# Attention scores by pairs of heads in two 64-row chunks, row maxima from the first chunk alone

## The reference

```python
x = x + tanh(g_xattn) * xattn(layernorm(x), ctx, ctx)            # softmax(q k^T / 4) v, 16 heads
x = x + tanh(g_ffn) * ffn(layernorm(x))
# in ffn: attn = softmax(rope(q) rope(k)^T / 4); sa = (attn v) Wo; x = rmsnorm(src + sa) * norm1_w
# then shared SwiGLU + two of eight experts per token, and a second rmsnorm
```

## Time and profile before

| | us |
|---|---|
| median of 3 runs | 788.73 (787.22 to 789.63) |
| profiled execution, its own time | 793.59 |
| its span, first to last instruction | 791.8 |
| first unit's exponential starts | 55.2 |
| last unit's exponential starts | 535.1 |
| TensorE clock, mean of full | 0.986 |

### The profile page before, as it was taken

The page is one execution under the profiler, slowest core; times in us unless marked ns, Lnnn a source line. Parts: engine busy times, 40 slices in busy tenths (PEclk is TensorE's granted clock), DMA queues, the critical chain, the costliest instruction groups (busy, mean ns, idle before and its releaser), DMA issues.

```text
span 791.8 us, 10350 instructions
## 1 busy us (share of the span) xinstructions
PE 746.5 (94%) x3510; PEld 342.7 (43%) x3510; DVE 512.4 (65%) x777; ACT 408.1 (52%) x766; POOL 225.6 (28%) x342
## 2 busy tenths in 40 slices
PE   5889999999999999999999999999999999989994
PEld 3432343243233233233323423425645755458883
DVE  2588847956978878878797798743366022623764
ACT  2437867777767767876675777683211122222000
POOL 3360222314315405304222410010105622400654
PEclk9989999999999999999999999999999999999997
DMA  7792334216215414513411341006003734000010
GB/s 233 207 256 57 81 84 144 79 32 204 63 50 164 122 41 126 141 41 94 146 43 40 125 112 47 1 2 213 0 0 125 272 115 133 0 1 1 34 41 34
DMA packets 51892, 73.31 MB, mean 93 GB/s; under 512 B 7808, under 2 KB 42880, under 8 KB 51840
## 3 DMA queue, kind: packets, MB, share of 16 engines
q1 hardware_dynamic: 47248, 63.80, 27.4%
q0 software_dynamic: 2816, 8.46, 2.8%
q10 hardware_dynamic: 1776, 0.40, 0.3%
HBM read 45.04 MB, written 27.33 MB: 91 GB/s over the span
## 4 chain that ended last, share of the span: by engine, by line
PE 75%; DVE 14%; ACT 5%; issue 3%; DMA 1%; POOL 1%; ACTq 0%; DVEq 0%; POOLq 0%
PE ps L1483 35%; PE ps L1629 12%; PE ps L1653 11%; PE ps L1603 10%; DVE negm L1136 7%; ACT hS L891 3%; PE ps L1478 2%; DVE bst L1014 2%; PE ps L1617 1%; PE ps L1542 1%; DMA bv_bc<-in_L_xattn_bv_dram 1%; PE ps L1537 1%; PE ps L1563 0%; POOL out_dram L753 0%; DVE rows L1021 0%
## 5 line engine op out<-in xcount | busy, mean ns | idle before, releaser
L1136 DVE TENSOR_REDUCE negm<-ps 128x2 f32<-128x1024 f32 x256 | 304.0, 1221 | 75.8 <-PE ps L1603 68.0
L891 ACT ACTIVATE hS<-ps 128x512 f32<-128x512 f32 x512 | 280.6, 604 | 116.2 <-PE ps L1653 114.4
L1653 PE MATMUL ps<-w 98*128 98x512 bf16 x512 | 170.6, 386 | 4.8 <-DVE qk L1069 1.9
L1603 PE MATMUL ps<-w 96*128 96x512 bf16 x512 | 154.9, 383 | 7.3 <-DVE negm L1136 6.4
L1629 PE MATMUL ps<-hS,mix 128*17 128x512 f32 x1024 | 134.7, 598 | 0.2
L1653 PEld LDWEIGHTS ps<-w 98*128 98x128 bf16 x512 | 44.0, 97 | 157.0 <-ACT hS L891 76.7
L1603 PEld LDWEIGHTS ps<-w 96*128 96x128 bf16 x512 | 47.9, 99 | 59.7 <-DVE negm L1136 13.2
L1335 DVE SCALAR_TENSOR_TENSOR ctxs<-qk,ps 128x512 f32<-128x512 f32 x32 | 22.0, 688 | 76.3 <-ACT qk L925 51.1
L925 ACT ACTIVATE qk<-ps 128x512 f32<-128x512 f32 x32 | 19.1, 597 | 82.5 <-PE ps L1483 78.6
L1483 PE MATMUL ps<-w,hS 128*128 x256 | 55.7, 379 | 2.0 <-issue 2.0
L1483 PEld LDWEIGHTS ps<-w,hS 128*128 128x128 f32 x256 | 48.6, 190 | 9.4 <-issue 2.9
(11 more groups left out here) (210 smaller groups left out, 875.5 us busy)
## 6 DMA issues: line engine op xcount, KB each, us to landing
w<-scrq SPq DMA_DIRECT2D x32, 384.0 KB, 4.5
scrk<-mix SPq DMA_DIRECT2D x24, 256.0 KB, 2.1
scrq<-mix SPq DMA_DIRECT2D x16, 384.0 KB, 3.3
scrq<-mix SPq DMA_DIRECT2D x24, 256.0 KB, 2.5
w<-scrk SPq DMA_DIRECT2D x32, 192.0 KB, 2.9
w<-scrk SPq DMA_DIRECT2D x32, 128.0 KB, 2.9
w<-in_L_ffn_W_experts_dram SPq DMA_DIRECT2D x8, 512.0 KB, 8.0
mix<-scrf SPq DMA_DIRECT2D x4, 528.0 KB, 5.5
```

The lines of the kernel that those rows point to most:

```text
L891: nc.scalar.activation(prob[:, kt % PROB_SLOTS, s % HG, :], slot_bank(("unit", u)), ACT.Exp, scale=SC).then_inc(s_exp, 1)
L1136: V.tensor_reduce(negm[:, gi % 2, h, 2 * t2:2 * t2 + 2], ps[:, bank:bank + 2, :], AX.X, ALU.max, negate=True).then_inc(s_re, 1)
L1603: last = MM(ps[:, bank + t, :], qs[0:STK, g, h, tt * P:(tt + 1) * P], ks[0:STK, g, h, :], start=True, stop=True)
L1653: MM(take(("unit", u)), ks[:, g, h, kt * P:(kt + 1) * P], qs[:, g, h, :], start=True, stop=True).then_inc(s_sT, 1)
```

## The change

Each unit's score becomes two accumulating matmuls over 64 and 34 rows, and two heads are taken together: the even head of a pair lies in partitions 0 to 63, the odd one in 64 to 127, so their matmuls use the upper and the lower half of the array and two different banks. The first chunk holds terms 0 to 3 (the larger ones in the new order of `Q_PART` and `K_PART`), the second terms 4 and 5 and the two maximum rows (for the even head it runs over 64 rows, zeros and ones included). The maxima come from the first chunk alone, for two heads and one tile of queries: two matmuls, each into its own bank, and DVE reduces each bank in an instruction of 128 x 512. There are four score banks (0, 1, 7, 5), and three banks for maxima (2, 3, 4), each single. `scrk` gets all six terms, stacks are loaded in eight DMAs a group instead of four, the set-up memsets cover other rows (SP waits for the first of them), the hook lists and three of the fixed steps are new.

```diff
-Q_PART = [0, 0, 0, 1, 1, 2]
-K_PART = [0, 1, 2, 0, 1, 0]
+Q_PART = [1, 1, 0, 0, 0, 2]
+K_PART = [1, 0, 1, 0, 2, 0]
+HALF = 64
 LEAD = 12
 PROB_SLOTS = 3
-AT_COPY, AT_HEADS, AT_MAX, AT_ROWS = 4, 8, 9, 11
-SCORE_BANKS = [0, 1, 7]
+AT_COPY, AT_HEADS, AT_MAX, AT_ROWS = 3, 9, 10, 11
+SCORE_BANKS = [0, 1, 7, 5]
+MAX_BANKS = [2, 3, 4]
...
-    KROWS = STK + MPART
+    assert HALF == 4 * DH and STK - HALF + MPART <= HALF
+    SECOND = [(0, HALF), (HALF, STK + MPART)]
+    TERMS2 = [(0, STK - HALF), (HALF + MPART, STK + MPART)]
+    M_ROWS = (HALF - MPART, HALF + MPART)
     PAIRS = NH * TT // 2
     UNITS = NH * TT
     STEPS = UNITS // NG
     KTS = NG * TT
-    SCR = [16 * 5, 16 * 3]
+    SCR = 16 * 5
+    HP = HG // 2
+    STACKED = 16 * 8
...
-    N_RING = N_PAIRS + GROUPS
+    N_RING = 2 * N_PAIRS + GROUPS
...
+    CROSS_STEPS = [("stats", 0, -34), ("norm", 1, -20), ("norm", 0, -16), ("tile", 2, -11), ("empty", 2, -11),
+        ("tile", 0, -11), ("empty", 0, -11), ("tile", 1, -8), ("empty", 1, -8), ("tile", 3, -7), ("empty", 3, -7),
+        ("tile", 4, -7), ("empty", 4, -5), ("tile", 5, -5), ("empty", 5, -4), ("tile", 6, -4), ("empty", 6, -4),
+        ("part0", 0, -3), ("rest", 0, -2), ("part1", 0, 2), ("empty", 8, 2), ("tile", 8, 2), ("part2", 0, 4),
+        ("tile", 7, 4), ("empty", 7, 4), ("part0", 1, 4), ("rest", 1, 5), ("tile", 9, 5), ("empty", 9, 5),
+        ("part1", 1, 8), ("part2", 1, 12)]
+    SELF_STEPS = [("stats", 0, -28), ("norm", 0, -21), ("norm", 1, -19), ("empty", 0, -15), ("tile", 0, -15),
+        ("tile", 1, -7), ("empty", 1, -6), ("empty", 2, -5), ("tile", 2, -5), ("tile", 4, -3), ("tile", 3, -3),
+        ("empty", 3, -3), ("empty", 4, -2), ("part0", 0, -1), ("tile", 5, -1), ("empty", 5, 0), ("sum", 0, 1),
+        ("tile", 6, 5), ("empty", 6, 5), ("tile", 7, 5), ("empty", 7, 5), ("rest", 0, 5), ("sum", 1, 6), ("rest", 1, 7),
+        ("tile", 8, 7), ("empty", 8, 7), ("part0", 1, 8), ("part2", 1, 9), ("part1", 0, 11), ("part2", 0, 11),
+        ("part1", 1, 15)]
+    FA_STEPS = [("fatile", 0, 16), ("faempty", 0, 16), ("fatile", 1, 17), ("faempty", 1, 17), ("fatile", 2, 20),
+        ("faempty", 2, 20), ("fatile", 3, 21), ("faempty", 3, 21), ("fastats", 0, 31), ("nf", 0, 41)]
...
-        SLOTS.append(("unit", u_))
+        if s_ % 2 == 0:
+            SLOTS.extend([("unit", u_), ("unit", u_ + 1)])
...
-        return ps[:, SCORE_BANKS[SLOT[key] % 3], :]
+        return ps[:, SCORE_BANKS[SLOT[key] % 4], :]
...
-        scrk = nc.dram_tensor("scrk", [2, NPART, DH * NH, L], BF16, kind="Internal").ap()
+        scrk = nc.dram_tensor("scrk", [2, NTERM, DH * NH, L], BF16, kind="Internal").ap()
...
-                return self.n - 1, 2 + 2 * ((self.n - 1) % 2)
+                return self.n - 1, MAX_BANKS[(self.n - 1) % 3]
...
-                    if X or Q_PART.count(part) == 1:
-                        d_ = (scrk[par, part] if X else scrq[par, Q_PART.index(part)]).rearrange("(o p) t -> p o t", p=P)
-                        sp.dma_start(d_, p_).then_inc(s_scr[X], 16)
+                    scr, terms = (scrk, K_PART) if X else (scrq, Q_PART)
+                    at = [r for r in range(NTERM) if terms[r] == part]
+                    if len(at) == 1:
+                        sp.dma_start(scr[par, at[0]].rearrange("(o p) t -> p o t", p=P), p_).then_inc(s_scr[X], 16)
                         return
-                    r = Q_PART.index(part)
-                    c = Q_PART.count(part)
+                    r0, dr = at[0], at[1] - at[0]
                     for o in range(2):
-                        d_ = scrq[par, r:r + c, o * P:(o + 1) * P].rearrange("r p t -> p r t")
-                        sp.dma_start(d_, p_[:, o, :].unsqueeze(1).to_broadcast([P, c, L])).then_inc(s_scr[0], 16)
+                        d_ = scr[par, r0:at[-1] + 1:dr, o * P:(o + 1) * P].rearrange("r p t -> p r t")
+                        sp.dma_start(d_, p_[:, o, :].unsqueeze(1).to_broadcast([P, len(at), L])).then_inc(s_scr[X], 16)
                 ready = (s_p0, s_p1, s_spl)
                 if n < 2:
@@ -531,24 +540,27 @@
                         put(0, part, ready[part])
                         put(1, part, ready[part])
-                def keys(g):
-                    row = 0
-                    for terms in range(NPART, 0, -1):
-                        sp.dma_start(ks[row:row + terms * DH, g], heads(scrk, terms, g)).then_inc(s_stk[g], 16)
-                        row += terms * DH
-
-                def heads(scr, terms, g):
-                    return scr[par, 0:terms].rearrange("r (d h) t -> (r d) h t", h=NH)[:, g * HG:(g + 1) * HG]
+                def get(X, g):
+                    scr = (scrq, scrk)[X][par]
+                    def terms(a, z, j):
+                        return scr[a:z].rearrange("r (d h) t -> (r d) h t", h=NH)[:, g * HG + j:(g + 1) * HG:2]
+                    for j in range(2):
+                        sp.dma_start(stacks[j * HALF:(j + 1) * HALF, X, 0, g], terms(0, 4, j)).then_inc(s_stk[g], 16)
+                    for j in range(2):
+                        a, z = TERMS2[j]
+                        sp.dma_start(stacks[a:z, X, 1, g], terms(4, NTERM, j)).then_inc(s_stk[g], 16)
                 for g in range(NG):
                     ge(sp, s_sT, ((n - 1) * NG + g + 1) * STEPS)
                     if g == 0:
-                        sp.wait_ge(s_scr[1], (n + 1) * SCR[1])
-                    keys(g)
+                        sp.wait_ge(s_scr[1], (n + 1) * SCR)
+                    get(1, g)
                     if g == 0:
-                        sp.wait_ge(s_scr[0], (n + 1) * SCR[0])
-                    sp.dma_start(qs[0:STK, g], heads(scrq, NTERM, g)).then_inc(s_stk[g], 16)
+                        sp.wait_ge(s_scr[0], (n + 1) * SCR)
+                    get(0, g)
...
+            sp.wait_ge(s_one, 1)
...
-            pool.memset(stacks[96:P, 1, NG // 2:], 1.0).then_inc(s_one, 1)
+            pool.memset(stacks[0:HALF + MPART, 1, 1], 1.0).then_inc(s_one, 1)
...
-            pool.memset(stacks[96:P, 1, 0:NG // 2], 1.0).then_inc(s_one, 1)
+            pool.memset(stacks[HALF // 2:HALF, 0, 1], 0.0).then_inc(s_one, 1)
...
-                act.dma_start(qs[STK:KROWS, gi % NG, :, :], mTs[:, gi % 2, :]).then_inc(s_mrow, 16)
+                if gi == 0:
+                    act.wait_ge(s_one, 2)
+                act.dma_start(stacks[M_ROWS[0]:M_ROWS[1], 0, 1, gi % NG], mTs[:, gi % 2, :]).then_inc(s_mrow, 16)
...
-                h, t2 = p // 2, p % 2
-                c, bank = ring.take()
-                dve.wait_ge(s_rf, c + 1)
-                V.tensor_reduce(negm[:, gi % 2, h, 2 * t2:2 * t2 + 2], ps[:, bank:bank + 2, :], AX.X, ALU.max,
-                                negate=True).then_inc(s_re, 1)
+                hp, tt = divmod(p, TT)
+                for j in range(2):
+                    c, bank = ring.take()
+                    dve.wait_ge(s_rf, c + 1)
+                    V.tensor_reduce(negm[:, gi % 2, j, hp, tt:tt + 1], ps[:, bank, :], AX.X, ALU.max, negate=True).then_inc(s_re, 1)
...
-                if k >= 3:
-                    emptied(SLOTS[k - 3])
+                if k >= 4:
+                    emptied(SLOTS[k - 4])
...
-                ge(pe, s_re, c - 1)
+                ge(pe, s_re, c - 2)
                 return bank
             def max_pair(q):
                 gi, p = divmod(q, PAIRS // NG)
                 g = gi % NG
-                h, t2 = p // 2, p % 2
+                hp, tt = divmod(p, TT)
                 if p == 0:
-                    pe.wait_ge(s_stk[g], (gi // NG + 1) * 64)
-                bank = ring_bank()
-                for t in range(2):
-                    tt = 2 * t2 + t
-                    last = MM(ps[:, bank + t, :], qs[0:STK, g, h, tt * P:(tt + 1) * P], ks[0:STK, g, h, :],
-                              start=True, stop=True)
-                last.then_inc(s_rf, 1)
+                    pe.wait_ge(s_stk[g], (gi // NG + 1) * STACKED)
+                for j in range(2):
+                    bank = ring_bank()
+                    a, z = j * HALF, (j + 1) * HALF
+                    MM(ps[:, bank, :], stacks[a:z, 0, 0, g, hp, tt * P:(tt + 1) * P], stacks[a:z, 1, 0, g, hp, :],
+                       start=True, stop=True).then_inc(s_rf, 1)
+            def score(u, i):
+                gi, s = divmod(u, STEPS)
+                g = gi % NG
+                kt, h = divmod(s, HG)
+                hp, j = divmod(h, 2)
+                a, z = SECOND[j] if i else (j * HALF, (j + 1) * HALF)
+                if s == 0 and i:
+                    pe.wait_ge(s_mrow, (gi + 1) * 16)
+                last = MM(slot_bank(("unit", u)), stacks[a:z, 1, i, g, hp, kt * P:(kt + 1) * P], stacks[a:z, 0, i, g, hp, :],
+                          start=(i == 0), stop=(i == 1))
+                if i:
+                    last.then_inc(s_sT, 1)
...
-                        if s == 0:
-                            pe.wait_ge(s_mrow, (gi + 1) * 16)
```

(34 more changed lines are left out.)

23 lines of the change are left out of this document (8 added, 15 removed).

## The result

The kernel after takes 794.91 us (median of 5 runs, 794.39 to 797.72), the kernel before on the same chip 789.43 (787.22 to 792.05): a ratio of 1.0081 (of the means) with a 95% interval of 1.0058 to 1.0104. The change makes the kernel slower, by 5.5 us between the medians and 6.4 by the ratio. The forecast was 785.6, 3 us faster. The profiled execution of after took 794.39 (span 792.7), that of before 793.59 (span 791.8).

A forecast was written before the change was run, and what follows sets the result against it. PE was taken to bound plain attention stretches, with PE, DVE or ACT hooks setting most others. Table -3.1, bank -4, row mode +3 and start +1 gave -3.1 us, so 785.6 against the median 788.73; range 765 to 811.

The forecast's parts named there:

- Scores and maxima in halves: Attention on PE: score pair stays 0.435 us, maxima 0.435 less a stretch, doubled weight loads hidden; PE's work 2.82 to 2.385.
- The rival without overlap: Halves of the array run in turn: plain stretch 3.69 us on PE, 878 us in total; chance 0.06.
- Reductions: DVE in attention: four one-bank reductions a stretch take 2.43 us back to back, 2.75 if each stands alone.
- my table: Prices each of 122 attention stretches as the longest of PE, DVE, ACT with hooks: 473.9 us before, 470.8 after.
- The ring: Three single maxima banks: fill 3 waits 0.52 us for reduction 0, so a plain stretch takes 2.90.
- the rival in which it does not bind: Reduction 0 returns before PE needs it: plain stretch 2.43 us, 768 us in total; chance 0.15.
- Row mode beside full rows: 118 whole-array blocks between half-row scores: 0.04 us extra each, +3 in all; bounds 0 to 0.32 a block.
- The fourth score bank: Attention: one more bank for scores removes waits that the table lacks, between 0 and -7 us; taken as -4.
- Before unit 0: Ahead of attention: queries' stack loads in four more DMAs start later, between 0 and +2 us; taken as +1.
- The reloads: Stack loads of later groups: four more issues and 6 MB more through DRAM stay hidden.
- The sum: Whole kernel: -3.1 by the table, -4 bank, +3 row mode, +1 start make -3.1 us, so 785.6.
- the second: Rival: switches between half rows and whole array cost 0.32 us a block, 797 in total, 806 with unhidden loads; chance 0.26.

The follow-up runs named there:

- The order that frees it: The kernel after reordered to scores, scores, maxima, values, maxima: 818.51 us, ratio 1.0379 to before; also with maxima 14 pairs ahead: 806.49 us, ratio 1.0195.
- the pairs with 64 rows: Projection products cut to 64 partitions in after and in before: ratios to before 1.0194 and 1.0242; only from the third instance on, 1.0047 and 1.0052.

## Why the prediction was wrong

- *Scores and maxima in halves.* Right: four scores in 0.44, two maxima in 0.21, and the doubled weight loads hidden in plain stretches. The rival without overlap is refuted.
- *Reductions.* Right in the plain stretch: 512 of 0.683, and from 195.49 four take 2.48, where I had 2.43. A little too low where hooks stand between them: the stretch with statistics is 3.94, 0.16 above my table's 3.78; four single ones (2.75) would have made it 4.10. The run with half reductions shows how much hangs on DVE: 26 us.
- *The ring.* Right: 0.52 of wait, a plain stretch of 2.90, and the rival in which it does not bind (2.43) is refuted. The order that frees it gives 2.47, half the reduction gives 2.64. That order still lost in the total, by its hooked stretches.
- *Row mode beside full rows.* This step failed: the term was mis-sized, since it went by the wrong row. I took 0.04 a block, +3 in all: 0.22 around the product with the values less 0.18 around a projection tile. Measured are up to 0.30 at a tile of four wide products, 0.14 at one of eight narrow ones, 0.24 at turned heads (0.10 and 0.14). The bounds held that (0 to 0.32), and twice my table's +4.4 at 0.1 would be +8.8 at 0.2 a block. The row that I subtracted was the wrong one: the tile of the earlier trace rows is one of eight narrow products and loses 0.18 by itself, while a tile of four wide ones (171.02 to 172.96, above) loses nothing. Against that one the columns' row says 0.22. A row of the very crossing stood in the trace of before, at the 16 tiles of 64 rows (239.76 to 241.13 above), and the count of 118 blocks did not tell these from the others. The rule of the Trainium skill, "TensorEngine Tiling (Array Packing)", section "Key Properties", that a change of the tiling mode drains TensorE, agrees with the 0.10 at each crossing and the weights that are not loaded ahead; I had set it aside by the same wrong subtraction.
- *The fourth score bank.* I took -4, "a little over half" of what the table could not explain, without a row. No such gain can be seen, and no run measures the bank by itself: PE's queue still waits for ACT 66.8 us in 85 to 460 us (53.6 for the scores of before), of which the matmuls' own records show 5.3, and one row of after has a wait of PE of 1.06 for a score bank (378.09). The run with three score banks shows that pairs need the fourth.
- *Before unit 0.* Forecast +1, measured -1.8: the first exponential at 53.4 and not 55.2. The size is not firm: in the run of after whose edit begins at the third instance it comes at 54.9, with the same code up to there. The reloads stayed hidden, as said: PE waits for a stack once, 1.33 us at 35.46, ahead of unit 0.
- *The sum.* Attention: forecast about -4 (-3.1, -4 and +3), measured +6.4. By the table the 10 us between would be 6 for crossings (+8.8 in place of +3) and 4 for the bank, but that is arithmetic, not a measurement. Measured are the product tiles alone, by the pairs with 64 rows: at most 4.4 us in after for 30 of them (2.5 for the 24 projection tiles), where the forecast had +3 for all 118 blocks. That 2.7 out of after and 4.1 into before make up the distance between the two kernels only says again that the edited ones take the same time; 4.1 is the price in before's order, and in after's it is 2.5. Of the rivals the second, told at 797 without unhidden loads, came nearest to 794.9; it had 0.32 a block and the -4 of the bank, so its nearness is in part luck.

What stays open: the other 2 us or so of the loss, or more, which lie among turnings, transposes, waits for score banks and the hooks' places, and no run parts them. By instances of 16 stretches (from product to product, before and after): 63.3 and 65.1, 62.8 and 64.6, then 59.4 and 59.0, 60.9 and 60.1, 60.8 and 60.0, then 67.0 and 68.1, 55.7 and 59.9 (1.3 of this the clock), and 45.5 and 46.1 for the last 15. So after is shorter in the three instances in which only projections of self-attention are made, and longer where those of cross-attention (the first two) and the output projections (the last three) stand. And whether the freed order (plain 2.47) would win with lists of hooks made for it was not tried; with lists made for the other it did not.

## What to carry to other kernels

Before splitting TensorE's rows, count the blocks that use the whole array in between: here each way over cost 0.10 us, and a tile of float32 products up to 0.30, over 30 tiles of products at most 4.4 us of the 6.4 that the kernel lost. Look for blocks that already cross in the kernel before: their rows have the price. Time taken off the engine that bounds a stage is a gain only as far as the buffers behind it come free: work out for each fill of a ring when its reduction returns, before and after the work gets shorter. And where a cost has no row, the nearest row is near only if it is of the same kind (rows, not columns), and a row that is subtracted must be of the same tile.

## What the runs showed of the hardware that was not expected

- A matmul of 64 rows after one of 96 to 128, or the other way round, starts 0.10 us late (197.90 to 198.22; the way back by the sum, 0.31 for three crossings), and its weights are not loaded ahead (PEld idle 0.23 in front of 198.21). From 98 to 128 rows, at a tile of four wide products, there is no such gap (0.22 from start to start, 171.02 to 171.24).
- A tile of four wide float32 products holds PE for 1.72 when it has 128 rows beside matmuls of 98 (171.24 to 172.96), and for 1.91 when one side has 64: 128 rows beside 64 (107.66 to 109.57, half of after's tiles) or 64 beside 98 (171.35 to 173.26).
- The two halves of the rows work for different operations too. In after, a product of self-attention on one half starts with a score on the other:

```profile
247.08 0.48 PE L1558 MATMUL ps<-fkv,cT 64*128 64x256 f32 x1
247.09 0.39 PE L1631 MATMUL ps<-w 64*128 64x512 bf16 x1
```

- With products of 64 rows ahead of unit 0, PE ran at half speed there for long, in both kernels: in before the clock granted over the first 54 us was 0.68 (0.95 with 128 rows), and the first product with the values came 10 us later; in after it came 16 us later with products at half their pace. With the same edit from the third instance on, the granted clock between first and last product stayed at 1.00.
- One stretch at half clock cost 1.27 us (4.18 for 2.91), in after at 474.8.
